# Local attention with 32 score columns a row, and experts' first tiles loaded singly

## The reference

```python
q = _rmsnorm(q, qn_w)
k = _rmsnorm(k, kn_w)
scores = jnp.einsum('bhqd,bhkd->bhqk', q, k) / jnp.sqrt(jnp.float32(D))
invalid = (col > row) | (row - col >= W)          # W = 32
scores = jnp.where(invalid, neg_inf, scores)
masked_attn = jnp.where(invalid, 0.0, jax.nn.softmax(scores, axis=-1))
gene_means = jnp.mean(jax.nn.sigmoid(masked_attn), axis=-1)
denom = gene_means + 0.5
sum_inv = jnp.sum(1.0 / denom, axis=2, keepdims=True)
fitness = 1.0 / (denom * sum_inv)
scores = scores + jnp.log(fitness)[..., None]
out = jnp.einsum('bhqk,bhkd->bhqd', jax.nn.softmax(scores, axis=-1), v)
```

## Time and profile before

| what | value |
|---|---|
| median of 3 runs | 1810.18 us (1806.8 to 1815.78) |
| profiled execution, its own time | 1825.79 us |
| its span (first to last instruction) | 1824.5 us |
| PE busy, matmul | 1262.5 us (69%) |
| DVE busy | 1238.5 us (68%) |
| ACT busy | 924.9 us (51%) |
| POOL busy | 536.9 us (29%) |
| mean granted clock of PE | 0.816 of full speed |

### The profile page before, as it was taken

The page is one execution under the profiler, slowest core; times in us unless marked ns, Lnnn a source line. Parts: engine busy times, 40 slices in busy tenths (PEclk is TensorE's granted clock), DMA queues, the critical chain, the costliest instruction groups (busy, mean ns, idle before and its releaser), DMA issues. The chain is left out here.

```text
span 1824.5 us, 41994 instructions
## 1 busy us (share of the span) xinstructions
PE 1262.5 (69%) x16223; PEld 649.9 (36%) x16223; DVE 1238.5 (68%) x3287; ACT 924.9 (51%) x1391; POOL 536.9 (29%) x995
## 2 busy tenths in 40 slices
PE   2755445445676778889997563776778799988746
PEld 2743444434653212222222252445222222222236
DVE  4348687752577789998775345257789999886234
ACT  0215622211234568887886423024467688888512
POOL 2321122204666341132013233166433100111323
PEclk9976555556856799999999778666599999999858
DMA  8410000002100110000000055000000000000012
GB/s 240 94 44 1 25 4 4 4 15 65 53 1 11 57 33 1 2 1 2 3 2 12 12 134 137 2 1 1 1 1 1 1 1 2 1 2 1 13 43 77
DMA packets 59365, 50.46 MB, mean 28 GB/s; under 512 B 7057, under 2 KB 54273, under 8 KB 58721
## 3 DMA queue, kind: packets, MB, share of 16 engines
q1 hardware_dynamic: 53488, 36.94, 7.8%
q0 software_dynamic: 4736, 9.74, 1.6%
q10 hardware_dynamic: 944, 1.10, 0.2%
HBM read 32.78 MB, written 18.38 MB: 28 GB/s over the span
## 5 line engine op out<-in xcount | busy, mean ns | idle before, releaser
L1609 ACT ACTIVATE arena<-psum 128x1024 f32<-128x1024 f32 (+3 forms) x640 | 560.7, 898 | 190.9 <-PE psum L1502 172.7
L1661 DVE TENSOR_REDUCE arena<-psum 128x1 f32<-128x512 f32 x768 | 480.0, 684 | 63.0 <-PE psum L1492 59.2
L1518 PE MATMUL psum<-arena 128*9 128x256 f32 (+2 forms) x4352 | 345.2, 394 | 0.9 <-POOL arena L1726 0.8
L1492 PE MATMUL psum<-arena 64*128 64x512 bf16 (+3 forms) x1280 | 241.0, 372 | 127.8 <-DVE arena L1661 58.2
L1666 DVE CUSTOM_DVE_ANT_0 arena<-psum,wqkv 128x384 bf16<-128x384 f32 (+3 forms) x512 | 230.5, 487 | 89.3 <-PE psum L1492 74.6
L1502 PE MATMUL psum<-arena 64*128 64x512 bf16 (+3 forms) x1280 | 232.5, 360 | 20.9 <-ACT arena L1609 15.2
L1492 PEld LDWEIGHTS psum<-arena 64*128 64x128 bf16 x1280 | 64.0, 94 | 384.3 <-DVE arena L1661 199.0
L1726 POOL TENSOR_SCALAR_AFFINE_SELECT arena<-arena 128x256 f32<-128x256 f32 x256 | 103.9, 408 | 324.5 <-ACT arena L1609 322.2
L1518 PEld LDWEIGHTS psum<-arena 128*9 128x9 f32 x4352 | 67.7, 89 | 172.7 <-issue 133.0
L1704 POOL CAST arena<-arena 128x16 bf16<-128x16 f32 x64 | 16.4, 257 | 326.0 <-DVE arena L1672 323.8
L656 DVE TENSOR_SCALAR small<-psum,YT 128x128 f32<-128x128 f32 x168 | 50.6, 343 | 84.6 <-PE psum L569 83.8
(11 more groups left out here) (332 smaller groups left out, 1974.8 us busy)
## 6 DMA issues: line engine op xcount, KB each, us to landing
arena<-taps SPq DMA_DIRECT2D x8, 1024.0 KB
big_w<-in_w SPq DMA_DIRECT2D x2, 2048.0 KB, 21.8
ACCn<-made_rows SPq DMA_DIRECT2D x16, 256.0 KB, 3.8
regions<-sorted_rows SPq DMA_DIRECT2D x5, 741.8 KB, 4.7
sorted_rows<-arena SPq DMA_DIRECT2D x2, 1483.5 KB, 15.8
ACCn<-sorted_rows SPq DMA_DIRECT2D x8, 258.0 KB, 3.4
ACCn<-regions SPq DMA_DIRECT2D x32, 64.5 KB, 1.8
w<-in_w SPq DMA_DIRECT2D x2, 1024.0 KB
```

The lines of the kernel that those rows point to most:

```text
L1492: pe.matmul(psum[:, b, 0:w], plain_q[v % 2][rows, a, i * P:(i + 1) * P], keys[rows, 2 * hq + a, c * GW:c * GW + w], start=True, stop=True) ...
L1518: mm = pe.matmul(psum[32 * hh:32 * hh + 9, O_BANK, lo:hi], values[:, tile_of(v, j), 4 * hq + hh, :], prob[(t + hh // 2) % N_PROB][:, hh % ...
L1609: act.activation(prob[t % N_PROB][:, :, off:GW], both, ACT.Exp, scale=INV_SQRT_HD).then_inc(a_got, 1)
L1661: dve.tensor_reduce(place, bank[:, 0:w], AX.X, ALU.max).then_inc(a_max_got, 1)
```

## The change

In local attention, the row with number i in its block needs the columns above i of the previous block's 32 and the columns up to i of its own. The new kernel puts both into the same 32 columns: ACT copies the previous block's half from PSUM (`first`), and DVE overwrites the places where the mask is not zero with the own half (`copy_predicated`). So a tile has 512 score columns a partition instead of 1024. The partitions now hold four heads (k) by 32 rows, and the free dimension holds (r, A, j) with head 8A + 2k + r and block j. After the transpose POOL multiplies the turned block by two 0/1 masks, `former` and `own`, which parts it again. The values are no longer made in the projection stage: ACT copies each block of YT four times side by side (`fourfold`), PE makes values of it per block (`new_values`), and ACT keeps for partitions of head group k only that group's columns, in four copies, in a buffer whose other places are zero. PE then weighs with 32 matmuls a tile, 128 partitions by 32 by 32. The value bias is added as a column when the rows are turned at the end, and is loaded as one row at the start of the score loop. The sum over rows uses a matrix with ones in 32x32 blocks; before the rows are scaled, 16 small matmuls and four DVE copies bring each head's share from (head, row) to (row, head).

In the experts, the first four tiles are loaded by one DMA each in all four stages, each with its own semaphore, and are turned and copied singly, alternating between banks 6 and 7. PE makes these four transposes before the first layer 1.

```diff
-        if c < 2:
-            sp.dma_start(rows_of_tiles(lo, hi), sorted_rows[c].rearrange("(s p) d -> p s d", p=P)[:, lo:hi, :]).then_inc(tile_in[q], 16)
-        else:
-            for s in chunk(c, q):
-                row = sp.value_load(tile_row[0:1, s:s + 1], min_val=0, max_val=(EXPERTS[c] - 1) * T + s * P)
-                sp.dma_start(rows_of_tiles(s, s + 1)[:, 0, :], regions[bass.ds(row, P), :]).then_inc(tile_in[q], 16)
+    for s in range(TILES[c]):
+        q = s // GT
+        landed = first_in[s] if q == 0 else tile_in[q]
+        if c >= 2:
+            row = sp.value_load(tile_row[0:1, s:s + 1], min_val=0, max_val=(EXPERTS[c] - 1) * T + s * P)
+            sp.dma_start(rows_of_tiles(s, s + 1)[:, 0, :], regions[bass.ds(row, P), :]).then_inc(landed, 16)
+        elif q == 0 or s % GT == 0:
+            end = s + 1 if q == 0 else chunk(c, q)[-1] + 1
+            sp.dma_start(rows_of_tiles(s, end), sorted_rows[c].rearrange("(s p) d -> p s d", p=P)[:, s:end, :]).then_inc(landed, 16)
 def made_back_sp(c):
     for k in range(2):
...
+    def turn_first(s):
+        pe.wait_ge(first_in[s], 16 * (c + 2))
+        if s >= 2:
+            pe.wait_ge(x_copied, copied(c, s - 2))
+        pe.transpose(psum[:, 6 + s % 2, 0:P], rows_of_tiles(s, s + 1)[:, 0, 0:D], ident[:]).then_inc(x_turned, 1)
...
-    turn_rows(0)
+    for s in range(GT):
...
+        act.wait_ge(x_turned, copied(c, tiles[0]))
+        dst = xt[q % 2][:, at:at + n]
         if scale_col is None:
-            act.activation(xt[q % 2][:, 0:n], psum[:, 6, 0:n], ACT.Copy).then_inc(x_copied, 1)
+            act.activation(dst, psum[:, bank, 0:n], ACT.Copy).then_inc(x_copied, 1)
         else:
-            act.activation(xt[q % 2][:, 0:n], psum[:, 6, 0:n], ACT.Identity, scale=scale_col).then_inc(x_copied, 1)
-    copy_rows(0)
+            act.activation(dst, psum[:, bank, 0:n], ACT.Identity, scale=scale_col).then_inc(x_copied, 1)
+    for s in range(GT):
+        copy_rows([s], 6 + s % 2)
     for s in range(n_tiles):
         act.wait_ge(layer1_made, tb + s + 1)
         if s >= 2:
...
     def project_sp():
-        for k, b in enumerate(("L0_attn_bq", "L0_attn_bk", "L0_attn_bv")):
-            sp.dma_start(bqkv[:, k * D:(k + 1) * D], on_all(ins[b], 0, D)).then_inc(w_bias_in, 16)
-        sp.wait_ge(w_values, NT)
-        sp.wait_ge(w_part, 6 * NG)
-        sp.dma_start(v_prev[W:P, :, :], v_own[0:P - W, :, :]).then_inc(v_shifted, 16)
-        sp.dma_start(v_prev[0:W, 1:NT, :], v_own[P - W:P, 0:NT - 1, :]).then_inc(v_shifted, 16)
...
             pool.wait_ge(w_scaled, g + 1)
             pool.tensor_tensor(rows, rows, qk_w[:, 1, :].unsqueeze(1).broadcast_to([P, GT * NH, HD]), ALU.mult).then_inc(w_weighed, 1)
...
-                dve.tensor_tensor(v_own[:, m, :], psum[:, i, 2 * D:3 * D], bqkv[:, 2 * D:3 * D], ALU.add).then_inc(w_values, 1)
+                dve.tensor_tensor(raw[:, :, i, :], both(psum[:, i, 0:2 * D]), both(bqk), ALU.add).then_inc(w_raw, 1)
...
+    wide = lambda k: take(k * K, GW).rearrange("p (x w) -> p x w", w=W)
+    score, prob = [wide(65 + 2 * i) for i in range(4)], [wide(73 + 2 * i) for i in range(2)]
+    former_t, own_t = [wide(77 + 2 * i) for i in range(2)], [wide(81 + 2 * i) for i in range(2)]
+    values = [take((85 + 2 * i) * K, GW).rearrange("p (j c) -> p j c", j=4) for i in range(4)]
+    same_k, bias_v = take(93 * K, P), take(93 * K + P, D)[0:1, :]
+    bias_col = take(94 * K + 3 * W, 1)
+    turned_mask, former, own = (take(94 * K + W * k, W) for k in range(3))
+    fourfold = [take((95 + 2 * i) * K, GW).rearrange("p (j k w) -> p j k w", j=4, k=4) for i in range(2)]
+    per_row = lambda k: take((104 + k) * K, NT * NH).rearrange("p (i x) -> p i x", i=NT)
     mx, ln_, rl, th, inv, fit, shift = (per_row(k) for k in range(1, 8))
+    heads_of = lambda cols, r, A: cols.rearrange("p (A k r d) -> p A r k d", A=2, k=4, r=2)[:, A, r, :, :]
+    PARTS = [slice(W * k, W * k + W) for k in range(4)]
+    sp.dma_start(bias_v, ins["L0_attn_bv"].unsqueeze(0)).then_inc(w_bias_in, 16)
+    pool.memset(take(85 * K, 4 * GW), 0.0)
+    own_pool(pool.memset(same_k, 0.0))
+    for k in range(4):
+        done = pool.memset(same_k[PARTS[k], PARTS[k]], 1.0)
+    done.then_inc(s_set_up, 1)
+    chain(dve.transpose(turned_mask, window_mask[:, 1, 0:W]))
+    dve.tensor_scalar(former, turned_mask, 0.5 * MASKED, None, ALU.is_ge).then_inc(s_set_up, 1)
+    dve.tensor_scalar(own, turned_mask, 0.5 * MASKED, None, ALU.is_lt).then_inc(s_set_up, 1)
     def score_pe():
...
-            for h in range(NH):
-                r = SLOT * (h % 2)
+            for A in range(2):
                 for j in range(4):
-                    t0 = m * P + j * W
-                    mm = pe.matmul(psum[W * j:W * j + W, b + h % 2, (h // 2) * 2 * W:(h // 2 + 1) * 2 * W],
-                                   queries[r:r + SLOT, h // 2, t0:t0 + W], keys[r:r + SLOT, h // 2, t0:t0 + 2 * W],
-                                   start=True, stop=True)
+                    for k in range(4):
+                        for r in range(2):
+                            rows, a, t0 = slice(SLOT * r, SLOT * r + SLOT), 4 * A + k, m * P + j * W
+                            mm = pe.matmul(psum[PARTS[k], b + r, (4 * A + j) * 2 * W:(4 * A + j + 1) * 2 * W],
+                                           queries[rows, a, t0:t0 + W], keys[rows, a, t0:t0 + 2 * W], start=True, stop=True)
             mm.then_inc(s_scored, 1)
+        def new_values(m):
+            bank = psum[:, 6 + m % 2, :]
...
+                pe.wait_ge(s_kept, m - 1)
+            pe.wait_ge(s_fourfold, m + 1)
+            for j in range(4):
+                mm = pe.matmul(bank[:, j * D:(j + 1) * D], fourfold[m % 2][:, j, :, :].rearrange("p k w -> p (k w)"),
+                               wqkv[:, 2 * D:3 * D], start=True, stop=True)
+            mm.then_inc(s_values, 1)
         def weighted_values(m):
-            pt, ob = prob_t[m % 2], 4 + m % 2
-            pe.wait_ge(s_turned, m + 1)
+            pe.wait_ge(s_cut, m + 1)
+            pe.wait_ge(s_kept, m + 1)
             if m >= 2:
                 pe.wait_ge(s_out, m - 1)
-            for h in range(NH):
-                s = (h % 2) * 8 + h // 2
-                for k, vals in enumerate((v_prev, v_own)):
-                    for j in range(4):
-                        q = slice(W * j, W * j + W)
-                        mm = pe.matmul(psum[q, ob, h * HD:(h + 1) * HD], pt[q, s, k * W:(k + 1) * W],
-                                       vals[q, m, h * HD:(h + 1) * HD], start=(k == 0), stop=(k == 1), skip_group_check=True)
+            for A in range(2):
+                for r in range(2):
+                    for former_one in (True, False):
+                        for j in range(4):
+                            t = 4 * m + j - former_one
+                            mm = pe.matmul(heads_of(psum[PARTS[j], 4 + m % 2, 0:D], r, A),
+                                           (former_t if former_one else own_t)[m % 2][:, 8 * r + 4 * A + j, :],
+                                           heads_of(values[t // 4 % 4][:, t % 4, :], r, A), start=former_one, stop=not former_one,
+                                           skip_group_check=True)
             mm.then_inc(s_weighed, 1)
-        pe.wait_ge(v_shifted, 32)
-        pe.wait_ge(v_padded, 1)
+        pe.wait_ge(w_bias_in, 48)
+        pe.matmul(psum[:, 4, 0:1], bias_v, ones[0:1, 0:1], start=True, stop=True).then_inc(s_set_up, 1)
         for m in range(NT + 2):
             if m < NT:
                 scores(m)
+                new_values(m)
             if m >= 2:
                 weighted_values(m - 2)
+    def both_halves(m):
+        return psum[:, 2 * (m % 2):2 * (m % 2) + 2, :].rearrange("p r (x w) -> p (r x) w", w=2 * W)
     def score_dve():
         def masked(m):
-            sc, b = score[m % 3], 2 * (m % 2)
-            dve.wait_ge(s_scored, m + 1)
-            if m >= 3:
-                dve.wait_ge(s_prob, m - 2)
-            dve.tensor_tensor(sc, psum[:, b:b + 2, :].rearrange("p k (h w) -> p (k h) w", w=2 * W),
-                              window_mask[:, min(m, 1), :].unsqueeze(1).broadcast_to([P, NH, 2 * W]), ALU.add).then_inc(s_masked, 1)
+            sc = score[m % 4]
+            dve.wait_ge(s_first, m + 1)
+            dve.copy_predicated(sc, window_mask[:, 1, 0:W].bitcast(U32).unsqueeze(1).broadcast_to([P, NH, W]),
+                                both_halves(m)[:, :, W:2 * W]).then_inc(s_masked, 1)
             dve.wait_ge(s_masked, m + 1)
+            if m == 0:
...
+            dve.tensor_tensor(sc, sc, bcast(mx[:, m, :], W), ALU.subtract).then_inc(s_below, 1)
...
             chain(dve.tensor_reduce(ln_[:, m, :], sc, AX.X, ALU.add))
             chain(dve.reciprocal(rl[:, m, :], ln_[:, m, :]))
             if m >= 2:
                 dve.wait_ge(s_weighed, m - 1)
-            dve.transpose(pt.rearrange("p h w -> p (h w)"), sc.rearrange("p h w -> p (h w)")).then_inc(s_turned, 1)
```

(50 more changed lines are left out.)

94 lines of the change are left out of this document (50 added, 44 removed).

## The result

The changed kernel took 1819.99 us (median of 13 runs, 1816.69 to 1825.07), the kernel before, run beside it, 1811.72 (13 runs). The ratio is 1.0046 [1.0033, 1.0059]: slower by some 8 us, less than the 0.5% that the forecast had set as the bound of "the same", and 8 us above the forecast of 1812 (the forecast had +1.6 us for the change, the runs show +8.3). The profiled execution took 1820.98 us, 1 us above its median.

A forecast was written before the change was run, and what follows sets the result against it. PE's supply of small instructions was taken to bound the old score loop, DVE close behind. Start +3.1, loop +9.5, fitness 0, projection -6.0, experts -5.0 made +1.6 us on 1810.18: 1812 us, range 1798 to 1831.

The forecast's parts named there:

- What bounds before: Old score loop: bound by how fast PE gets small instructions, 9.6 us a tile, with DVE close behind at 7.65.
- The ring: New score loop: DVE's masked pass, POOL's cuts and product, ACT's tanh and next first copy close a turn of 9.85 us.
- rival A: The forecast itself: the ring paces the score loop near 9.85 us, projection and experts give that back; 1812 us, chance 0.47.
- 0.1 overlaps each time: ACT's part of the turn: each successive ACT copy overlaps its neighbour by 0.1 us, within 1.76 us, 1.8 with hops.
- The score stage: Local attention's second stage: start +3.1, loop 154.9 us against 145.4 (+9.5), fitness net 0.
- Fitness net 0: Fitness step after the score loop: -2.2 us from PE's vanished backlog, +2.2 from the new spreading over heads.
- -1.1 without the third: Projection stage: DVE's start waits for two bias DMAs instead of three, saving 1.1 us.
- -1.6 in each: Last two expert stages: L569 starts at 62.25 instead of 63.86 because three tiles are turned before the fourth lands.
- For chunks needed 8 us later: 0: First two expert stages: SP's further issues come 1.5 us later, for chunks needed 8 us later, costing nothing.
- B: Slower, score loop: POOL's cuts take 1.75 us each, +16 us, total +17.6, 1828 us; chance 0.28.
- C: Faster, score loop: products at 0.95 us without waits, turn 9.1 us, start hidden, about -11 us, 1799 us; chance 0.15.
- D: Score loop: the ring does not close, DVE paces at about 5 us a tile, -68 us, 1744 us; chance 0.05.

The follow-up runs named there:

- e6: The kernel before, without the weighted values of 8 of its 16 heads, part of the result left out: 1796.49 us, ratio 0.9858.
- e3: The changed kernel with POOL's product with the reciprocal issued before the two cuts, same instructions: 1778.45 us, ratio 0.9816 to the kernel before.
- e4: The changed kernel with ACT's fourfold and first copies of the next tile issued right behind exp, ahead of tanh: 1761.46 us, ratio 0.9724 to the kernel before.
- e9: The changed kernel with POOL's first cut issued twice in each tile: 1840.10 us, ratio 1.0156 to the kernel before.
- e10: The changed kernel with three of ACT's four kept copies left out from tile 4 on: 1822.90 us, ratio 1.0054 to the kernel before.
- e5: The changed kernel with both reorderings, POOL's product ahead of the cuts and ACT's next fourfold and first behind exp: 1762.25 us, ratio 0.9670 to the kernel before.
- e8: The kernel with both reorderings, with ACT awaiting POOL's large zero fill only before the first kept copy: 1762.28 us, ratio 0.9670 to the kernel before.
- e7: The changed kernel with the projection's third bias load, value columns and value-bias additions put back, results unused: 1833.48 us, ratio 1.0068 to the kernel before.
- e2: The changed kernel with the experts' loading as before: 1825.15 us, ratio 1.0067 to the kernel before.
- e1: The kernel before with only the experts' first tiles loaded, turned and copied singly, attention as before: 1809.73 us, ratio 0.9984.

## Why the prediction was right, and where its numbers were off

**What bounds before** was right: halving the weighted values moved the loop from 9.28 to 7.45 us a tile (e6), where the forecast had 7.65 for DVE's part. Its "9.85 us a tile, against 8.64" sets a full turn against a mean with the short first tiles; turn against turn it was 10.08 against 9.28. The sum is not touched, since it goes by the 145.4 us of the whole loop.

**The ring** (rival A, 0.47) is what happened, shown by e3 (cuts out: -2.54 us a turn), e4 (ACT's order changed: the turn spans two tiles), e9 (a cut more: +1.34 a turn) and e10 (copies beside it: nothing). Its terms, forecast and measured: DVE 4.45 and 4.47; POOL 3.6 and 3.64; the predicated copy 0.69 and 0.73, a single pass; ACT 1.8 and 1.97. The step that was off is "0.1 overlaps each time": out starts 0.65 us behind a tanh of 0.63 (263.65 and 264.30), not before its end. In e4 the same two start 0.53 apart; why is open. Sum 10.08 against 9.85.

**The score stage.** Start +3.07 (forecast +3.1). The loop is 159.0 us against 154.9: first turn 5.87 (5.4), the next two 9.38 and 9.49 (9.1 and 9.25), twelve turns of 10.08 and 0.16 once, 121.2 (118.2), tail 13.07 (12.95). So the term was mis-sized by 4.1 us, three of it by 0.23 a turn. Fitness net 0, as forecast, by other amounts: -2.2 from the waits of L1069 (2.90 to 0.68), +0.94 from L1065, the rest by L1107 and L1084. L1065 is held by POOL. In ten profiles it starts beside POOL's addition of 4.5 us (L1130) and ends 0.14 to 0.16 us after it, whether 2.1 or 3.0 us of it were left; in e3, e5 and e8 it starts beside a cut, takes 1.30 us and ends as shortly behind the cut. Alone the same form takes 0.29 us (L1073). The forecast had taken over its time of before, 2.25 us.

**The projection** saved some 7 us, forecast 6.0. Over the profiles counted at e7, the wait for the biases fell by 2.1 us in the mean and the stage behind it by 5.1 (three profiles at 86.8 to 87.8 us, nine at 81.0 to 83.1); the forecast had 1.1 and 4.9. So "-1.1 without the third" is the term that was too small: it took the two landing times, 5.6 and 4.9 us, and one issue of 0.43 as the price of a third DMA. Why an issue of 0.43 us holds its waiter 2.1 us longer is not shown.

**The experts.** In the runs they brought 2.9 us (0.9 to 4.9), forecast 5.0. The step "-1.6 in each" held: L587 after SP's first issue 7.08 to 5.50 and 7.18 to 5.41, and in the first stage 4.81 to 3.54. "For chunks needed 8 us later: 0" is not refuted either: from L587 on the third stage took 60.2 us instead of 59.8, but over the four stages nothing of the gain is given back. From SP's first issue to its first load of the made rows they take 234.5 to 235.7 us together in three profiles with the old loading (before, e2, e6) and 227.4 to 229.8 in ten with the new one, 6.2 less in the mean. Why the runs show less than these stages stays open.

**The sum.** Attention was forecast at +6.6 us. From e1 to the changed kernel the next stage starts 8.3 us later (376.02 and 384.34): projection -7.8, start +3.1, loop +14.2, fitness -0.4, and -0.7 ahead of the projection, which the change does not touch. Over the profiles, attention from its first bias issue to the next stage took 264.4 and 265.9 us before and 273.4 to 274.6 in four with the new one, +8.7 in the mean. With the experts' -6.2 the parts that the change touches cost 2.5 us, near the forecast's 1.6. The runs say +8.3 (6.0 to 10.7). What remains of a profiled execution outside these parts took 1313 to 1324 us (1323 before, 1318 in the changed kernel) and differs between executions by more than this gap of 6 us, so no profile shows where it lies. So the ring and the loop's length are shown, and of the 7 us between forecast and measurement the stages explain 1; the rest stays open. The measured time lies in the forecast's range, and the width of that range (33 us) had a part in it.

**The rivals.** B (cuts of 1.75 us) did not happen: a cut took 1.26, forecast 1.25, by interpolating between the earlier trace rows on the length of a run. By the Trainium skill (GPSIMD Engine Reference, section 3.1), a product of 512 was estimated at 1.12 us; L1023's product, with a single value per run, took 1.05, the cuts 1.26, so the page's figure is near but does not tell them apart. C (products at 0.95 us, a ring of 9.1) did not happen either: the product took 1.05 and the ring 10.08. D, where DVE sets the pace, did not happen with ACT's order as written. But e4 and e5 show how close it lay: the same instructions in another order turn a kernel 0.5% slower than before into one 3.3% faster. The forecast's PE part, 4.1 to 5.5 us a tile (its upper figure, 128 pairs at 30 ns and eight at 0.23 us, adds up to 5.7), came out at its lower end: in the turn above L948 starts at 255.16 and the last score pair is issued by 259.36.

## What to carry to other kernels

Cutting the work of every engine in a loop helps only if the new dependences leave the engines apart: before costing instructions, follow one tile's result through each engine's program order until it comes back, and add up that ring; its length over the number of tiles that it spans is the pace. In such a ring the order of issue is worth more than the instructions (e3: 2.5 us a tile for two lines moved), and once one ring is opened the next must be looked for (e5: from ACT's order to PE's). A loop bound by many small matmuls is the best place to take matmuls away, but the gain is only what lies down to the next bound, 1.8 us a tile here (e6). And a mean over a loop that has short first turns is not its turn: compare turn with turn.
